# Second selective scan of a two-layer kernel: the sum over states by accumulating DMAs instead of GpSimd additions

## The chip, the cores and the metric

The kernel runs on one core of a Trainium2 chip. The metric is device time in microseconds (us) of one launch; every time below is one core's. The engines are named as in the profile: PE (TensorE matmul), PEld (its weight loads), DVE (VectorE), ACT (ScalarE), POOL (GpSimd), SP (SyncE, which here only issues DMAs); a name with a q (SPq, ACTq, POOLq) is an engine's issuing side.

## What is computed

Two layers run on x (4 sequences of 512 tokens, width 512) and on a context of width 256. Each layer has a selective scan on the context, whose result is gated with x and added to it, and a feed-forward part: in the first layer a mixture of 16 experts (4 chosen for each token) with a shared expert, in the second a ternary-weight block. The part that the change touches is the sum over the 16 states in the second layer's scan:

```python
def step(state, xs):
    d_t, B_t, C_t, u_t = xs
    dA = jnp.exp(d_t[..., None] * A)
    state = state * dA + (d_t * u_t)[..., None] * B_t[:, None, :]
    y_t = jnp.einsum('ben,bn->be', state, C_t)
    return (state, y_t)
...
y = y + D[None, :, None] * u
y = y * jax.nn.silu(z)
```

## The kernel before

The stages run one after another: the first scan (tiles named `ssm_`) beside the splitting of the expert weights, gate and routing (`gate_`), the experts together with the second scan (`moe_`), and the last block (`ffn_`). The change is in the third stage alone.

The second scan. For a batch b the 512 inner channels are 4 chunks of 128 partitions, and a half is 2 chunks. A step s is one half and one of the 16 states n; a batch has 32 steps, and the halves alternate (even steps half 0, odd steps half 1). In a step ACT writes the decay `dA` (two `act_exp` activations, L372), DVE the input `bu` (L449) and then the scan into `hs[:, j]` with j = s % 4 (`dve_scan`, L458; 128 partitions x 1024 f32, 512 KB), and POOL multiplies `hs[:, j]` in place by C (`pool_step`, L491). `pool_add` (L481) then adds `hs[:, j]` to its half of `U`, which held the scan's input u times D (`pool_y_init`, L473) and becomes y. There is one `U` (`dbl` is 1) and there are four `hs` buffers (`R` is 4). Semaphores: `prod_done` counts products, `acc_done` counts additions and starts at 4, and a scan of step s waits for `acc_done` at s + 1, which is the addition of step s - 4.

The slots. The stage is a loop of 168 slots, written out in the same order for every engine, and each slot has work of the experts and one entry of the scan: of a batch's 42 entries the first 10 (`PRO`) prepare the batch (projection, convolution, delta), and the other 32 are its steps. Slots 0 to 87 belong to the shared expert, and 88 to 167 to the 80 tiles of the chosen experts; so the steps of batches 0 and 1 lie beside the shared expert, and those of batches 2 and 3 beside the chosen ones. POOL's queue in a slot is: in the second kind of slot the gather of expert input for the tile after next (`fetch`, L1346, an indirect DMA that POOL issues, 256 KB), then `pool_add` of the step before, then `pool_step` of this one. In a batch's last slot a second `pool_add` follows for step 31.

Around it, `fetch(g + 2)` reads into `xg[:, g % 2]`, which PE transposes (`x_transpose`, L1418) in the next slot. ACT's convolution of the next batch (`act_conv`) writes into `hs` buffers 0 and 1 and waits for additions; ACT issues the store of y (`store_y`, L232) in the third preparing slot of the next batch, for the last batch after its last instruction of the stage. SP loads the weights of an expert as two DMAs of 1088 KB (L1324) and, beside the shared expert, the last block's weights in pieces of 512 KB (L1152).

Of the kernel before, what the change touches and what calls it, by code (L numbers as in the profile page):

```python
# [9 lines left out]
ALU = mybir.AluOpType  # L10
# [9 lines left out]
DI, NS, DC, DR = 512, 16, 4, 16  # L20
# [20 lines left out]
R = 4  # L41
# [4 lines left out]
STEPS = 2 * NS  # L46
# [34 lines left out]
class Mem:  # L81


    def __init__(self, nc, ctx, tag):
        self.nc, self.ctx, self.tag, self.sems = nc, ctx, tag, []
# [20 lines left out]
class Ssm:  # L106
# [10 lines left out]
    def __init__(self, nc, m, l, d, dbl, ring, alone):  # L117
        self.alone = alone
        self.nc, self.l, self.d, self.dbl, self.ring = nc, l, d, dbl, ring
        nsel = NS if alone else 2 * NS  # L120
        self.sel = m.sb("sel", [96, nsel, P], BF16)
        self.cx = m.sb("cx", [P, 2, L])
        self.w_in = m.sb("w_in", [P, 2, DI])
        self.w_x = m.sb("w_x", [P, KC, 96 + DR])
        self.w_up = m.sb("w_up", [P, DI])
        self.cw = m.sb("cw", [P, KC, DC])
        self.cb = m.sb("cb", [P, KC])
        self.db = m.sb("db", [P, KC])
        self.alog = m.sb("alog", [P, KC, NS])
        self.A = m.sb("A", [P, KC, NS])  # L130
        self.Dv = m.sb("Dv", [P, KC])
        self.ident = m.sb("ident", [P, P])
        self.U = m.sb("U", [P, dbl, KC, L])
        self.dlt = m.sb("dlt", [P, dbl, KC, L])
        self.du = m.sb("du", [P, dbl, KC, L])
        self.bc3 = m.sb("bc3", [96, dbl, L], BF16)
        self.low = m.sb("low", [P, L])

        self.Cs = m.sb("Cs", [P, NS if alone else 2, L])
        self.dA = m.sb("dA", [P, ring, HC, L])  # L140
        self.hs = m.sb("hs", [P, R, HC, L])
        if alone:
            self.diagD = m.sb("diagD", [P, KC, P])
        if not alone:
            self.acc = self.hs[:, 0:2, :, :].rearrange("p a b t -> p (a b) t")
            self.tmp = self.hs[:, 2:4, :, :].rearrange("p a b t -> p (a b) t")
        else:
            self.acc = m.sb("acc", [P, KC, L])[:]
            self.tmp = m.sb("tmp", [P, KC, L])[:]


        self.nbu = 2 if alone else 1
        self.bu = m.ps("bu", [P, self.nbu, HC, L])
        self.pB = m.ps("pB", [P, L])
        self.pC = None if alone else self.pB
        self.pY = [m.ps(f"pY{k}", [P, L]) for k in range(HC)] if alone else None
        self.pw = [m.ps("pw", [P, L])[:], self.bu[:, 1, 1, :]] if alone else [self.bu[:, 0, k, :] for k in range(2)]

        self.loaded = m.sem("loaded")
        self.cx_in = m.sem("cx_in")  # L160
        self.a_exp = m.sem("a_exp")
        self.a_neg = m.sem("a_neg")
        self.diag_rdy = m.sem("diag_rdy")
        self.in_rdy = m.sem("in_rdy")
        self.conv_a = m.sem("conv_a")
        self.conv_v = m.sem("conv_v")
        self.u_rdy = m.sem("u_rdy")
        self.xp_rdy = m.sem("xp_rdy")
        self.dts_rdy = m.sem("dts_rdy")
        self.bc_split = m.sem("bc_split")  # L170
        self.dtz_rdy = m.sem("dtz_rdy")
        self.ar_rdy = m.sem("ar_rdy")
        self.e_rdy = m.sem("e_rdy")
        self.t_rdy = m.sem("t_rdy")
        self.q_rdy = m.sem("q_rdy")
        self.ln_rdy = m.sem("ln_rdy")
        self.d_step = m.sem("d_step")
        self.b_rdy = m.sem("b_rdy")
        self.c_rdy = m.sem("c_rdy")
        self.c_evac = m.sem("c_evac")  # L180
        self.cf_rdy = m.sem("cf_rdy")
        self.cd_in = m.sem("cd_in")
        self.cs_in = [m.sem(f"cs_in{n}") for n in range(NS if alone else 0)]
        self.exp_rdy = m.sem("exp_rdy")
        self.bu_done = m.sem("bu_done")
        self.scan_done = m.sem("scan_done")
        self.prod_done = m.sem("prod_done")
        self.acc_done = m.sem("acc_done")
        self.sum_done = m.sem("sum_done")
        self.y_init = m.sem("y_init")  # L190
        self.y_out = m.sem("y_out")
        self.y_dram = m.sem("y_dram")
# [33 lines left out]
    def store_y(self, sp, y_ssm, b):  # L226

        if self.alone:
            sp.wait_ge(self.y_out, 2 * b + 2)
        else:  # L230
            sp.wait_ge(self.acc_done, (b + 1) * STEPS + R)
        sp.dma_start(y_ssm[b * L:(b + 1) * L, :].rearrange("(k p) n -> p k n", p=P),  # L232
                     self.U[:, b % self.dbl, :, :]).then_inc(self.y_dram, 16)

# [83 lines left out]
    def act_conv(self, act, b, c):  # L318
        act.wait_ge(self.in_rdy, b * KC + c + 1)
        if b:  # L320
            act.wait_ge(self.d_step, self.d_count(b, 0))
            if not self.alone:

                act.wait_ge(self.acc_done, b * STEPS + R - 3 + c // 2)
        self.nc.scalar.activation(self.acc[:, c, :], self.bank(b, c), ACT.Identity,
                                  bias=self.cb[:, c:c + 1], scale=self.cw[:, c, DC - 1:DC]).then_inc(self.conv_a, 1)

# [124 lines left out]
    def dve_scan(self, dve, s, j):  # L452

        q = j % self.ring
        dve.wait_ge(self.sum_done if self.alone else self.acc_done, s + 1)
        dve.wait_ge(self.exp_rdy, s + 1)
        dve.wait_ge(self.bu_done, s + 2)
        self.nc.vector.tensor_tensor_scan(self.hs[:, j, :, :].rearrange("p k t -> p (k t)"),  # L458
                                          self.dA[:, q, :, :].rearrange("p k t -> p (k t)"),
                                          self.bu[:, s % self.nbu, :, :].rearrange("p k t -> p (k t)"),  # L460
                                          0.0, ALU.mult, ALU.add).then_inc(self.scan_done, 1)


    def pool_start(self, pool):
        pool.sem_inc(self.prod_done, R)
        if not self.alone:
            pool.sem_inc(self.acc_done, R)

    def pool_y_init(self, pool, b):

# [6 lines left out]
    def pool_add(self, pool, b, half, s, j):  # L477
        Y = self.U[:, b % self.dbl, half * HC:(half + 1) * HC, :]
        pool.wait_ge(self.prod_done, s + 1 + R)
        pool.wait_ge(self.acc_done, s + R)  # L480
        self.nc.gpsimd.tensor_tensor(Y, Y, self.hs[:, j, :, :], ALU.add).then_inc(self.acc_done, 1)  # L481

    def pool_step(self, pool, s, j):
        pool.wait_ge(self.scan_done, s + 1 + self.ring)
# [1801 lines left out]
```

## Time and profile before

| | us |
|---|---|
| median of 3 runs | 2147.91 (2143.99 to 2150.92) |
| the profiled execution, its own time | 2147.24 |
| its span in the trace | 2145.4 |
| PE busy | 1639.1 (76%) |
| DVE busy | 1722.0 (80%) |
| ACT busy | 1205.2 (56%) |
| POOL busy | 1332.6 (62%) |
| the additions, L481, 128 of them | 302.0 (2.36 each) |
| the products of the same scan, L491, 128 of them | 301.6 (2.36 each) |

A busy time counts an instruction's own duration and no waits. Shares over the whole span mix stages with different limits: the steps of the second scan lie at 853 to 1013, about 1070 to 1240, 1320 to about 1525 and 1614 to 1823 us from the start of the span, and only what bounds those stretches matters here. DMAs of every engine's queue run on the same 16 DMA engines in this profile, and a share of DMA is the mean busy share of these 16.

### The profile page before, as it was taken

How to read it: one execution, taken by the hardware profiler on the slowest of the kernel's cores; microseconds unless marked ns; L12 is line 12 of the kernel's file. 1: busy time of each engine (PE TensorE's matmuls, PEld its weight loads, DVE VectorE, ACT ScalarE, POOL GpSimd, SP SyncE). 2: the span in 40 equal slices, each digit the busy share in tenths (PEclk: the TensorE clock that was granted, in tenths of full speed). 3: DMA queues.
4: the chain of work that ended last, by engine and by line, in shares of the span. 5: the costliest groups of instructions: out<-in, count | busy, mean ns of one | idle time of the engine just before them, and what ended most of it. 6: DMA issues, size and time to landing. Idle time of an engine off the chain costs nothing. (4 is left out here: it accounts for less than half of the span.)

```text
span 2145.4 us, 27108 instructions
## 1 busy us (share of the span) xinstructions
PE 1639.1 (76%) x8419; PEld 929.2 (43%) x8442; DVE 1722.0 (80%) x2275; ACT 1205.2 (56%) x1863; POOL 1332.6 (62%) x646
## 2 busy tenths in 40 slices
PE   4465765766664568888888889999999999157788
PEld 1121322222224435666556655666555666023344
DVE  2999999999977645998599947888658888578876
ACT  5776766675643116666666626555465555146576
POOL 2578888788983001998089924888518888663221
PEclk7787988889995569999999999999999999579999
DMA  7537546446546122332322242434444632542200
GB/s 260 196 129 232 178 145 220 165 150 202 177 137 256 69 81 69 110 97 71 106 79 84 72 168 100 167 128 177 152 162 154 213 109 70 178 138 63 74 21 30
DMA packets 121399, 289.21 MB, mean 135 GB/s; under 512 B 22801, under 2 KB 32273, under 8 KB 117073
## 3 DMA queue, kind: packets, MB, share of 16 engines
q1 hardware_dynamic: 86800, 206.73, 28.2%
q0 software_dynamic: 11520, 37.76, 6.0%
q10 hardware_dynamic: 22944, 43.00, 5.4%
q8 instruction: 77, 1.26, 0.2%
q14 instruction: 58, 0.47, 0.1%
HBM read 198.97 MB, written 88.47 MB: 134 GB/s over the span
## 5 line engine op out<-in xcount | busy, mean ns | idle before, releaser
L491 POOL TENSOR_TENSOR ssm_hs<-ssm_hs,ssm_Cs 128x1024 f32<-128x1024 f32 x128 | 313.8, 2461 | 89.3 <-DVE ssm_hs L458 89.3
L491 POOL TENSOR_TENSOR moe_hs<-moe_hs,moe_Cs 128x1024 f32<-128x1024 f32 x128 | 301.6, 2356 | 56.5 <-DVE moe_hs L458 55.6
L458 DVE TENSOR_TENSOR_SCAN moe_hs<-moe_dA,moe_bu 128x1024 f32<-128x1024 f32 x128 | 292.6, 2286 | 22.7 <-ACT moe_dA L372 14.6
L481 POOL TENSOR_TENSOR moe_U<-moe_U,moe_hs 128x1024 f32<-128x1024 f32 x128 | 302.0, 2360 | 6.3
L1445 PE MATMUL moe_pgu<-all_Wreg,moe_xt 128*128 x1920 | 305.1, 313 | 0.0
L458 DVE TENSOR_TENSOR_SCAN ssm_hs<-ssm_dA,ssm_bu 128x1024 f32<-128x1024 f32 x128 | 291.7, 2279 | 0.1
L304 PE MATMUL ssm_pY<-ssm_hs,ssm_ident 128*128 128x512 f32 x512 | 273.0, 661 | 8.6 <-POOL ssm_hs L491 8.5
L1395 PE MATMUL moe_pgu<-all_Wreg 128*128 128x256 f16 x2112 | 252.4, 277 | 3.1 <-DVE moe_hsl L1647 2.8
L1395 PEld LDWEIGHTS moe_pgu<-all_Wreg 128*128 128x128 f16 x2112 | 209.9, 100 | 54.6 <-issue 11.6
L1445 PEld LDWEIGHTS moe_pgu<-all_Wreg,moe_xt 128*128 128x128 f16 x1920 | 188.0, 98 | 96.2 <-issue 2.3
L743 POOL TENSOR_TENSOR ssm_wlo<-ssm_wst,ssm_whi 128x1360 f16<-128x1360 f32 (+2 forms) x63 | 189.2, 3003 | 44.8 <-ACT ssm_wst L678 44.8
L372 ACT ACTIVATE ssm_dA<-ssm_dlt,ssm_A 128x511 f32<-128x511 f32 x256 | 167.9, 709 | 62.0 <-DVE ssm_hs L458 58.9
L282 PE MATMUL ssm_pB<-ssm_bc,ssm_sel 96*128 96x512 bf16 x128 | 55.0, 430 | 170.4 <-DVE ssm_bu L449 170.3
L372 ACT ACTIVATE moe_dA<-moe_dlt,moe_A 128x511 f32<-128x511 f32 x256 | 169.9, 714 | 16.7 <-DVE moe_du L437 16.7
L473 POOL TENSOR_TENSOR moe_U<-moe_U,moe_Dv 128x2048 f32<-128x2048 f32 x4 | 14.4, 3598 | 252.7 <-DVE moe_du L437 252.7
L449 DVE TENSOR_TENSOR ssm_bu<-ssm_du,ssm_pB 128x1024 f32<-128x1024 f32 x128 | 157.0, 1227 | 13.6 <-PE ssm_pB L282 4.2
L1346 POOL DMA_INDIRECT moe_xg<-xn_d,all_idx x80 | 79.3, 991 | 132.5 <-PE moe_px L1418 122.7
L449 DVE TENSOR_TENSOR moe_bu<-moe_du,moe_pB 128x1024 f32<-128x1024 f32 x128 | 156.1, 1220 | 1.3 <-PE moe_pB L282 1.1
L304 PEld LDWEIGHTS ssm_pY<-ssm_hs,ssm_ident 128*128 128x128 f32 x512 | 108.3, 213 | 103.5 <-issue 84.5
L1426 PE MATMUL moe_pys<-all_Wreg,moe_hth 128*128 (+1 forms) x480 | 144.3, 382 | 10.1 <-DVE moe_htl L1665 10.1
L282 PEld LDWEIGHTS ssm_pB<-ssm_bc,ssm_sel 96*128 96x128 bf16 x128 | 12.9, 100 | 269.6 <-DVE ssm_bu L449 254.5
L1546 ACT ACTIVATE moe_sgs<-moe_pgu 128x352 f32<-128x352 f32 x80 | 37.1, 463 | 161.9 <-PE moe_pgu L1445 161.9
(274 smaller groups left out, 3298.8 us busy)
## 6 DMA issues: line engine op xcount, KB each, us to landing
ssm_wst<-in_w_all SPq DMA_DIRECT2D x51, 680.0 KB, 4.9
y_d<-moe_yo ACTq DMA_DIRECT2D x80, 256.0 KB
all_Wreg<-w_hi SPq DMA_DIRECT2D x16, 1088.0 KB
all_Wreg<-w_lo SPq DMA_DIRECT2D x16, 1088.0 KB
w_hi<-ssm_whi SPq DMA_DIRECT2D x51, 340.0 KB, 2.3
w_lo<-ssm_wlo SPq DMA_DIRECT2D x51, 340.0 KB, 3.1
ssm_Cs<-c_d SPq DMA_DIRECT2D x64, 256.0 KB, 5.3
all_Wreg<-w_sh SPq DMA_DIRECT2D x11, 768.0 KB, 9.0
```

The source lines that it names most:

```text
L282: self.nc.tensor.matmul(self.pB[:], self.sel[:, ds(n, 1), :], self.bc3[:, b % self.dbl, :], start=True, stop=True).then_inc(self.b_rdy, 1)
L304: mm = self.nc.tensor.matmul(self.pY[k][:], self.ident[:], self.hs[:, j, k, :], start=False, stop=last, skip_group_check=True)
L372: ex = nc.scalar.activation(self.dA[:, q, k, 1:L], self.dlt[:, b % self.dbl, c, 1:L], ACT.Exp, scale=self.A[:, c, ds(n, 1)])
L449: self.nc.vector.tensor_tensor(self.bu[:, s % self.nbu, :, :], self.du[:, b % self.dbl, half * HC:(half + 1) * HC, :], self.pB[:].unsqueez ...
L458: self.nc.vector.tensor_tensor_scan(self.hs[:, j, :, :].rearrange("p k t -> p (k t)"), self.dA[:, q, :, :].rearrange("p k t -> p (k t)"), ...
L481: self.nc.gpsimd.tensor_tensor(Y, Y, self.hs[:, j, :, :], ALU.add).then_inc(self.acc_done, 1)
L491: self.nc.gpsimd.tensor_tensor(self.hs[:, j, :, :], self.hs[:, j, :, :], self.Cs[:, i:i + 1, :].to_broadcast([P, HC, L]), ALU.mult)\
L743: nc.gpsimd.tensor_tensor(wlo[:, k, 0:n], wst[:, k, 0:n], whi[:, k, 0:n], ALU.subtract).then_inc(lo_rdy, 1)
L1346: nc.gpsimd.indirect_dma_start(out=xg[:, g % 2, :], out_offset=None, in_=r["xn_d"], in_offset=bass.IndirectOffsetOnAxis(ap=r["idx"][:, g:g ...
L1395: mm = nc.tensor.matmul(pgu[u % 2][:, q * TS:(q + 1) * TS], Ws[:, shared_place(c), z, o:o + P], xs[:, t % 2, k, :], start=(k == 0 and z == ...
L1426: mm = nc.tensor.matmul(py[:], ht[0:n, q, :], w_of(w, z, n, HK * 2 * IE + q * H, H), start=(q == 0 and z == 0 and ht is hth), stop=(q == 2 ...
L1445: mm = nc.tensor.matmul(ps, xt[:, g % 2, k, :], w_of(w, z, P, k * 2 * IE + o, IE), start=(k == 0 and z == 0 and xt is xth), stop=(k == HK ...
```

## The change

`pool_add` becomes a DMA from `hs[:, j]` to its half of `U`, both in SBUF, with an addition at the destination, issued by POOL. In place of `acc_done` there is a semaphore for each half, `acc_in[half]`, which every such DMA raises by 16 when it has landed. A DMA waits for the one before it of its own half, that is of step s - 2; a scan waits for the DMA of step s - 4; the store of y and the convolution of the next batch wait for both semaphores.

```diff
-        self.acc_done = m.sem("acc_done")
+        self.acc_in = [m.sem(f"acc_in{h}") for h in range(2)]
...
         else:
-            sp.wait_ge(self.acc_done, (b + 1) * STEPS + R)
+            for h in range(2):
+                sp.wait_ge(self.acc_in[h], 16 * (b + 1) * NS)
...
-                act.wait_ge(self.acc_done, b * STEPS + R - 3 + c // 2)
+                act.wait_ge(self.acc_in[0], 16 * (b * NS - 1))
+                act.wait_ge(self.acc_in[1], 16 * (b * NS - 2 + c // 2))
...
-        dve.wait_ge(self.sum_done if self.alone else self.acc_done, s + 1)
+        if self.alone:
+            dve.wait_ge(self.sum_done, s + 1)
+        elif s >= R:
+            dve.wait_ge(self.acc_in[s % 2], 16 * ((s - R) // 2 + 1))
...
         pool.sem_inc(self.prod_done, R)
-        if not self.alone:
-            pool.sem_inc(self.acc_done, R)
...
         pool.wait_ge(self.prod_done, s + 1 + R)
-        pool.wait_ge(self.acc_done, s + R)
-        self.nc.gpsimd.tensor_tensor(Y, Y, self.hs[:, j, :, :], ALU.add).then_inc(self.acc_done, 1)
+        if s >= 2:
+            pool.wait_ge(self.acc_in[half], 16 * (s // 2))
+
+        pool.dma_start(Y, self.hs[:, j, :, :], accum_op=ALU.add).then_inc(self.acc_in[half], 16)
```

POOL's queue beside the chosen experts, before: a gather, an addition that waits for the addition before it, a product that waits for its scan, and again (the gather's semaphore has the name that its number had in the first stage).

```order
L1346 DMA moe_xg<-xn_d,all_idx 128x512 [waits ssm0_y_out]
L481 TENSOR_TENSOR moe_U<-moe_U,moe_hs 128x1024 [waits moe_acc_done,moe_prod_done]
L491 TENSOR_TENSOR moe_hs<-moe_hs,moe_Cs 128x1024 [waits moe_c_evac,moe_scan_done]
L1346 DMA moe_xg<-xn_d,all_idx 128x512 [waits ssm0_y_out]
L481 TENSOR_TENSOR moe_U<-moe_U,moe_hs 128x1024 [waits moe_acc_done,moe_prod_done]
L491 TENSOR_TENSOR moe_hs<-moe_hs,moe_Cs 128x1024 [waits moe_c_evac,moe_scan_done]
```

The same place of POOL's queue in the changed kernel.

```order
L1351 DMA moe_xg<-xn_d,all_idx 128x512 [waits ssm0_sum_done]
L486 DMA moe_U<-moe_hs 128x1024 [waits moe_acc_in1,moe_prod_done]
L496 TENSOR_TENSOR moe_hs<-moe_hs,moe_Cs 128x1024 [waits moe_c_evac,moe_scan_done]
L1351 DMA moe_xg<-xn_d,all_idx 128x512 [waits ssm0_sum_done]
L486 DMA moe_U<-moe_hs 128x1024 [waits moe_acc_in0,moe_prod_done]
L496 TENSOR_TENSOR moe_hs<-moe_hs,moe_Cs 128x1024 [waits moe_c_evac,moe_scan_done]
```

No instruction has changed its place. The addition is now a DMA on the same queue as the gathers, with the gather of each slot ahead of it, and its wait is for a DMA of two steps before (`acc_in0` and `acc_in1` in turn), ahead of the product.

## Rows read from the trace of the kernel before

**Rows 1.** Busy time by engine in three stretches of steps (columns in the first line).

```profile
core 0: us, PE busy (x) PEld busy (x) DVE busy (x) ACT busy (x) POOL busy (x), PEclk, DMA share, GB/s
900.00:1000.00 100.00, 88.29 (x638) 62.33 (x637) 94.50 (x111) 63.15 (x122) 94.11 (x41) 0.98 0.29 90
1350.00:1500.00 150.00, 150.00 (x947) 94.63 (x945) 128.50 (x163) 80.51 (x173) 131.28 (x70) 1.00 0.44 156
1640.00:1800.00 160.00, 159.15 (x1005) 100.48 (x1004) 136.37 (x170) 85.47 (x185) 139.68 (x74) 1.00 0.44 149
```

**Rows 2.** The additions: durations, and the lists of waits before and behind them.

```profile
L481 POOL TENSOR_TENSOR moe_U<-moe_U,moe_hs x128: 2339/2359/2377, 858.2 to 1822.9; 128x1024 f32<-128x1024 f32 x128
its engine sat idle before it (us, times) until:
who waited for it (us, times):
busy tenths in 40 slices 0000000000000000444034400333203333000000
```

**Rows 3.** Timeline of one slot beside the shared expert.

```profile
908.49 2.29 DVE L458 TENSOR_TENSOR_SCAN moe_hs<-moe_dA,moe_bu 128x1024 f32<-128x1024 f32 x1 [0.27 <-ACT moe_dA L372]
908.50 2.35 POOL L481 TENSOR_TENSOR moe_U<-moe_U,moe_hs 128x1024 f32<-128x1024 f32 x1
...
910.69 0.40 DVE L1639 SCALAR_TENSOR_TENSOR moe_sgs<-moe_sgs,moe_pgu 128x256 f32<-128x256 f32 x1
910.85 2.35 POOL L491 TENSOR_TENSOR moe_hs<-moe_hs,moe_Cs 128x1024 f32<-128x1024 f32 x1
911.12 0.43 DVE L1642 SCALAR_TENSOR_TENSOR moe_pgu<-moe_pgu,moe_sgs 128x256 f32<-128x256 f32 x1
...
911.59 0.37 ACT L1532 CAST moe_hsh<-moe_pgu 128x256 f16<-128x256 f32 x1 [1.40 <-DVE moe_pgu L1642]
911.86 1.33 ACT L372 ACTIVATE moe_dA<-moe_dlt,moe_A 128x511 f32<-128x511 f32 x2
...
913.28 2.29 DVE L458 TENSOR_TENSOR_SCAN moe_hs<-moe_dA,moe_bu 128x1024 f32<-128x1024 f32 x1 [0.27 <-ACT moe_dA L372]
```

**Rows 4.** Timeline of one slot beside the chosen experts.

```profile
1646.12 0.99 POOL L1346 DMA_INDIRECT moe_xg<-xn_d,all_idx  x1
...
1647.00 0.60 PE L1418 MATMUL moe_px<-moe_ident,moe_xg 128*128 128x128 f32 x4
1647.12 2.37 POOL L481 TENSOR_TENSOR moe_U<-moe_U,moe_hs 128x1024 f32<-128x1024 f32 x1
...
1650.13 2.35 POOL L491 TENSOR_TENSOR moe_hs<-moe_hs,moe_Cs 128x1024 f32<-128x1024 f32 x1 [0.64 <-DVE moe_hs L458]
...
1652.64 0.98 POOL L1346 DMA_INDIRECT moe_xg<-xn_d,all_idx  x1 [0.15 <-issue]
...
1653.73 0.60 PE L1418 MATMUL moe_px<-moe_ident,moe_xg 128*128 128x128 f32 x4
```

**Rows 5.** What PE waited for beside batches 2 and 3 (us, times, longest).

```profile
PE moe_px L1418 <- DMA moe_xg<-xn_d,all_idx: 2.5, 2, 1.6
```

**Rows 6.** DMA from 1646 to 1652 us in 40 slices: a gather and a store.

```profile
DMA  0000000000007972799899961000000000000000
...
q0 software_dynamic: 80, 0.26, 14.5%
q10 hardware_dynamic: 144, 0.26, 11.7%
```

**Rows 7.** DMA issues beside the shared expert (last column: issue to landing).

```profile
wq_d<-moe_tq ACTq DMA_DIRECT2D x24, 256.0 KB, 2.0
...
moe_yo<-in_w_gate SPq DMA_DIRECT2D x5, 512.0 KB, 3.7
```

**Rows 8.** SP's waits for an expert's weights to land.

```profile
SPq L1326 <- DMA all_Wreg<-w_lo: 129.9, 15, 10.4
```

**Rows 9.** Timeline at the end of the stage.

```profile
1822.91 2.34 POOL L481 TENSOR_TENSOR moe_U<-moe_U,moe_hs 128x1024 f32<-128x1024 f32 x1
...
1828.00 0.45 ACTq L232 DMA_DIRECT2D y_ssm<-moe_U  x1
1837.41 0.34 SPq L1838 DMA_DIRECT2D ffn_ident<-in_ident_bf  x1
```

## The prediction, made before the changed kernel ran

> **What bounds the kernel now.** I read the busy time by stretch first, then the list of who waits for the additions, then the timeline of one slot of each kind.
>
> Beside the chosen experts (batches 2 and 3) PE is busy 150.00 of 150 us and 159.15 of 160 [rows 1]: it sets the pace, one slot in 1652.64 - 1646.12 = 6.52 us [rows 4], and POOL has slack: its product idles 0.64 us until the scan ends [rows 4]. Beside the shared expert (batches 0 and 1) no engine is full: DVE is busy 94.50, POOL 94.11 and PE 88.29 of 100 us [rows 1]. There the slot is a loop of DVE and ACT. From one scan's start to the next: 2.20 us to L1639, 0.43 to L1642, 0.47 to ACT's cast, 0.27 to the decays and 1.42 until these are done and the next scan starts, together 4.79 [rows 3]. The scan's last wait is for ACT, 0.27 us. POOL's addition and product take 2.35 each and, with 0.08 us between product and addition, also fill 4.79 [rows 3], but POOL follows the scan and no engine holds for it: under "who waited for it" of the additions stands nothing [rows 2]. So 302 us of POOL's time go away where they cost nothing.
>
> **The change part by part.**
>
> *Removed:* 128 additions of 2.36 us [rows 2]. Nobody waited for them, so 0. Lower bound of the effect: if POOL does hold the loop after all, see the third rival.
>
> *Added on POOL:* 128 issues. The trace has no such issue; the nearest row is the gather's, 0.99 us [rows 4]. Beside the shared expert POOL then has 1.0 + 2.35 = 3.4 us in a slot of 4.79, beside the chosen experts one gather more, 4.3 of 6.52. Even twice that issue time fits (4.4 and 5.3). The cover is POOL's slack behind the scan; without it each further us would go to every step. 0 us.
>
> *Added on the DMA engines:* per step 512 KB that is read, added and written from SBUF to SBUF. The trace shows neither an accumulating nor an SBUF-to-SBUF transfer. In the window of a slot the store of 256 KB from SBUF takes 11.7% of 6 us, 0.70 us of all 16 engines, the gather 14.5%, 0.87 us [rows 6]; so one pass of 512 KB is 1.4 us by the store and 1.7 by the gather. An addition must read source and destination: two passes, 2.8 us, if the write overlaps the reads as it does in a store. Lower bound, one pass: 1.4. Upper bound, three passes one after another: 4.2. I take 2.8, because reads and writes overlap in every transfer shown. The engines are otherwise busy 0.29 x 4.79 = 1.4 us of a slot beside the shared expert and 0.44 x 6.52 = 2.9 beside the chosen ones [rows 1], so they get to 4.2 of 4.79 and to 5.7 of 6.52. They hold, with little to spare.
>
> The Trainium skill ("Collectives: The Full Stack", the part on the bandwidth ceiling) says that an addition inside a DMA engine costs nothing by itself, but needs a second source read on the same ring, so that it goes at half the rate of a copy. No row here shows it; by it the transfer would be the same 2.8 us, and the three passes of the upper bound would be out.
>
> *From issue to landing.* The gather issued at 1646.12 has its first bytes moving in the 13th of 40 slices of 0.15 us, at 1647.8, 1.7 us after the start of its issue [rows 4, 6]. A store of 256 KB lands 2.0 us after its issue [rows 7], 1.3 more than its 0.70 on the engines; a load of 512 KB from HBM lands after 3.7, 2.3 more than its pass of 1.4. The new transfer ends in SBUF but comes from SBUF too, so I take the store's 1.3; with the load's 2.3 the landing is at 6.8. So an accumulating DMA lands 1.7 + 2.8 + 1.3 = 5.8 us after its issue starts; bounds 4.4 and 7.2. If a load of equal weight runs beside it, its 2.8 double: 8.6.
>
> *The new waits.* DMA s waits for DMA s - 2 of its half, two slots before: 9.58 us beside the shared expert, 13.0 beside the chosen ones, against 5.8 to 8.6. Behind the waiting DMA on POOL stand the product of the next step and the next gather; for the product wait the DMA after it, the copies of C and four steps later the scan, for the gather waits PE. Nothing of it moves while the landing stays under 9.58. A scan waits for the DMA of s - 4, issued some 14 us before: 0. The convolution of the next batch and the stores of batches 0 to 2 come three slots or more after the DMAs that they wait for: 0. With them the extra cost of the steps is 0.
>
> *The gathers* go ahead of the DMA of their slot and behind that of the slot before, 5.5 us older. From a gather's issue to its transposes are 1653.73 - 1646.12 = 7.6 us [rows 4], and it needs 1.7 + 0.87 + 1.3 = 3.9; PE waited for one only twice, 2.5 us in all [rows 5]. 0 us; the third of the mechanisms that make it slower is here.
>
> *The end.* The one place with no slot after it: the last addition ran from 1822.91 to 1825.25, ACT issued the store of y at 1828.00, and the next stage opened at 1837.41, after that store [rows 9]. The last DMA is issued at 1822.9 and lands at 1822.9 + 5.8 = 1828.7: the store goes 0.7 us later (bounds 0 and, with 7.2, 2.1), and the stage with it.
>
> **Sum.** 0 for the steps + 0.7 for the end. Against the profiled execution's own 2147.24 us that is 2147.9; its own time is 0.67 below the median of the runs, 2147.91, so I predict 2148.6.
>
> The Trainium skill ("DMA: Bandwidth & Descriptors", Anatomy of one DMA) gives 2.0 us plus the bytes at 436 GB/s, which makes an estimate of 4.4 us for two passes of 512 KB and, with 1.0 for the issue, 5.4; by it the end term would be 0.3 instead of 0.7. No row here shows the constant.
>
> **The rivals.**
>
> 1. *The DMA engines run full.* For it: 0.29 and 0.44 of them are already in use [rows 1], and beside an expert's two weight loads they have no room. It decides from 3.4 us of engine time per addition beside the shared expert (4.79 - 1.4) and 3.6 beside the chosen ones. At the upper bound of 4.2 the slots become 5.6 and 7.1 us: 64 x 0.8 + 64 x 0.6 = about 88 us, 2236. Against: it needs reads and writes that don't overlap. Chance 0.22.
>
> 2. *The chain of a half.* Engine time is there, but a DMA takes over 9.58 us to land, and POOL stands in its wait with the product behind it. With doubled transfers of the upper bound, 1.7 + 8.4 + 1.3 = 11.4, a step takes 5.7 instead of 4.79: 64 x 0.9 = 58 us, 2206. For it: latency per DMA is the least known term. Against: 7.2 alone, even at the bound. Chance 0.10.
>
> 3. *Late gathers.* While an expert's weights load (15 waits, 129.9 us, 8.7 each, the longest 10.4 [rows 8]) the DMA before a gather needs 8.6 us instead of 5.8, is still 3 us from done when the gather is queued behind it, and the gather shares too: 3.9 + 0.9 + 3 = 7.8 against 7.6. PE, the bound there, would wait perhaps 1 us per gather in the load, and each load covers one or two: some 16 us, 2164. Against: it is at the edge, and loads cover only part of the slots. Chance 0.12.
>
> 4. *Faster: POOL holds the loop beside the shared expert.* For it: its 2.35 + 2.35 + 0.08 are the very 4.79 of the slot, and scan and addition start within 0.01 us of each other [rows 3]. Freed, the slot would fall to DVE's busy share, 0.945 x 4.79 = 4.53: 64 x 0.26 = 17 us, 2131. It decides if the scans start on an addition; against it stands that the list of its waiters is empty [rows 2] and that the DVE and ACT loop closes by itself. Chance 0.08.
>
> **How the numbers follow.** The forecast, no change beyond the end term, has 0.48, with a range of its own of 2144 to 2153. Differences up to 0.3% (6.4 us) a measurement of this kernel can't tell from none. Faster is rival 4, 0.08. Slower are rivals 1 and 2 and most of rival 3, 0.42. The rest, 0.50, is the same. The range reaches down to 2141 and up to the bound of the first rival, 2236; outside lie rival 4 and what is worse than my bounds, together under 0.2.
>
> **What would show it.** POOL's busy time falls by about 302 us less the issues, 1 us each (or by all, if these aren't counted); the share of its queue q0 rises by 128 x 2.8 us; the slot in a timeline stays 4.79 and 6.5; the scans still wait last for ACT; no wait of POOL for a DMA; the store at 1828.7 on this clock. Wrong is it if POOL waits for the accumulating DMA, if the DMA share in the steps is near 1, or if the products start at once and the slot is under 4.79.

## The result, and the profile after

The changed kernel takes 2165.2 us (median of 5 runs, 2163.0 to 2168.1) against 2150.9 for the kernel before on the same chip: a ratio of 1.0076, 95% interval 1.0057 to 1.0094. It is slower by 0.76%, some 16 us (the two medians are 14.3 us apart). The forecast was no change (2148.6). The time lies within the stated range, outside of the likeliest case's own, 2144 to 2153, and at the size of the third rival, late gathers (2164).

The changed kernel in the three stretches of [rows 1], busy time by engine:

```profile
core 0: us, PE busy (x) PEld busy (x) DVE busy (x) ACT busy (x) POOL busy (x), PEclk, DMA share, GB/s
900.00:1000.00 100.00, 88.33 (x639) 62.38 (x638) 94.50 (x111) 63.29 (x122) 64.55 (x40) 0.98 0.87 197
1350.00:1500.00 150.00, 144.81 (x897) 89.52 (x895) 122.05 (x155) 77.30 (x165) 96.11 (x66) 1.00 0.84 228
1640.00:1800.00 160.00, 157.00 (x978) 97.65 (x975) 132.46 (x166) 82.60 (x178) 102.41 (x70) 1.00 0.86 236
```

POOL lost 30 of 100 us, as it should. Beside the shared expert nothing else moved: DVE has its 94.50 again. Beside the chosen experts PE, which sets the pace there, is no longer full: 144.81 of 150 where it had 150.00. The DMA share went from 0.29 beside the shared expert and 0.44 beside the chosen ones to 0.87 and to 0.84 and 0.86; the prediction's sums were 4.2 of 4.79 and 5.7 of 6.52, 0.88 and 0.87.

The new transfers, those that waited for one, and the queue of POOL in the page:

```profile
L486 POOL DMA_DIRECT2D moe_U<-moe_hs x128: 870/890/1108, 858.6 to 1841.2; - x128
...
  DVE moe_hs L463: 5.7, 22
  POOL moe_hs L496: 2.3, 1
  POOL moe_xg L1351: 0.3, 2
...
q0 software_dynamic: 29952, 104.88, 22.6%
```

An issue takes 0.89 us. The queue's share was 6.0% of 2145.4 us before, so one accumulating DMA of 512 KB takes (0.226 x 2163.1 - 0.060 x 2145.4) / 128 = 2.8 us of all 16 engines, the term that was assumed. The 22 waits of scans are in the place where they waited for ACT before, 0.27 us each, and cost nothing: the 64 scans beside the shared expert start within 0.1 us of those of before. Of POOL's one wait for an add, 2.3 us at 1718.45, the product's own scan explains all but 0.03 us.

**Where the time went.** I laid the starts of TensorE's `down` (L1431, the experts' second product, early in each slot) of both timelines side by side. By the clock of the kernel before, the changed kernel is 0.04 us behind at 1332 us, 10.0 behind at 1535 (end of batch 2), 9.9 at 1609, 12.7 at 1638 and 18.1 at 1821. What PE waited for in that part, after:

```profile
PE moe_px L1423 <- DMA moe_xg<-xn_d,all_idx: 5.4, 7, 1.6
PE moe_pys L1431 <- issue: 3.7, 8, 1.3
PE moe_pB L283 <- issue: 1.3, 5, 0.4
```

The first line is [rows 5] with seven waits in place of two. The other two have no counterpart before. One late gather in the timeline:

```profile
1352.80 1.06 POOL L1351 DMA_INDIRECT moe_xg<-xn_d,all_idx  x1 [0.16 <-issue]
...
1353.66 0.60 PE L1423 MATMUL moe_px<-moe_ident,moe_xg 128*128 128x128 f32 x4
1353.82 1.01 POOL L486 DMA_DIRECT2D moe_U<-moe_hs  x1
...
1361.60 0.66 PE L1423 MATMUL moe_px<-moe_ident,moe_xg 128*128 128x128 f32 x4 [1.04 <-DMA moe_xg<-xn_d,all_idx]
```

The gather issued at 1352.80 feeds the transposes of the next slot, 8.8 us later where 7.6 was the slack, and the weights of an expert load in these same microseconds. Ahead of it in POOL's queue stood an add that was issued together with these loads:

```profile
1347.23 0.32 SPq L1329 DMA_DIRECT2D all_Wreg<-w_hi  x1
...
1347.32 1.02 POOL L486 DMA_DIRECT2D moe_U<-moe_hs  x1
```

The trace's semaphore events tell when it landed: 12.7 us after its issue, where an add beside the shared expert took 5.4 (median). Each of the six gathers that made PE wait in batch 2 stood behind such an add. These six adds took 12.0 to 13.2 us, had 6.4 to 7.7 us to go when the gather was issued, and the gather landed 1.2 to 1.8 us after them, 8.0 to 9.0 us after its own issue. (The seventh wait is at 1545 us, between the batches, where the kernel before has one too.) In the window from 1353 to 1362 us the DMA engines are 90% busy or nearly so in most slices:

```profile
DMA  9899899697998989989949999699899896998999
...
q0 software_dynamic: 314, 1.16, 56.8%
q1 hardware_dynamic: 162, 1.14, 31.7%
q10 hardware_dynamic: 281, 0.51, 15.6%
```

q0 carries POOL's transfers, q1 the weights, q10 the stores of `y_d`. Six slots of batch 2 with such a wait each came out 0.9 to 1.6 us longer, 7.8 together; 4.8 of this lie ahead of the transposes, and 2.9 behind them, where the second kind of loss sits. This second kind has no releaser:

```profile
1696.80 1.50 PE L1450 MATMUL moe_pgu<-all_Wreg,moe_xt 128*128 x9
...
1699.62 0.23 PEld L1431 LDWEIGHTS moe_pys<-all_Wreg,moe_hth 128*128 128x128 f16 x2 [1.68 <-issue]
1699.63 0.60 PE L1431 MATMUL moe_pys<-all_Wreg,moe_hth 128*128 x2 [1.32 <-issue]
```

TensorE has ended one slot and begins the next 1.3 us late, though nobody it waits for is late. Between L1450 and L1431 (or L283) stand in its program the two reads of the routing table `tab` from SBUF into registers (`value_load`, which weights and which place). Most of these gaps are 0.2 to 0.4 us. The trace has the reads themselves, with their duration in ns (min/median/max), before and then after:

```profile
L1473 PEldq TENSOR_LOAD <-all_tab x80: 296/316/1004, 1259.2 to 1812.9; - x80
L1474 PEldq TENSOR_LOAD <-all_tab x80: 294/302/566, 1260.0 to 1813.6; - x80
```

```profile
L1478 PEldq TENSOR_LOAD <-all_tab x80: 296/608/1675, 1259.2 to 1830.8; - x80
L1479 PEldq TENSOR_LOAD <-all_tab x80: 295/666/1237, 1260.0 to 1832.1; - x80
```

A read takes twice as long beside the adds. Ahead of the gap above, the second read alone took 1.24 us. And there is a third piece, the clock at the start of batch 3, after and then before:

```profile
1628.00:1638.00 10.00, 9.44 (x42) 5.57 (x43) 6.70 (x10) 2.80 (x6) 8.55 (x6) 0.68 0.45 109
```

```profile
1628.00:1638.00 10.00, 10.00 (x67) 6.44 (x66) 8.93 (x12) 4.86 (x12) 8.43 (x5) 1.00 0.87 328
```

TensorE was granted 0.68 of its 2.4 GHz there, so it spent part of the stretch at 1.2; the slot took 2.8 us more. It had waited 3.1 us for DVE just before, in both kernels. Three runs below without a DMA add in this place fell too: 0.75 over 10 us with the adds beside the shared expert alone, 0.93 over 10 with no add, 0.89 over 30 in the kernel before with the table as constants. So I count these 2.8 us of the profile's 17.7 as no part of the change.

The last DMA add was issued at 1841.25 and the store of y at 1846.17, 4.9 us later; in [rows 9] it was 5.1 after the addition's start. The last add had landed at 1845.8, before the store. The end costs nothing.

### The profile page after: what moved, and what is told of

The parts are those of the page before. It is cut to its first block and busy times, and to the rows that moved or that the text cites. A ratio compares the mean times of both kernels' runs of the same rounds, so it can differ in the third digit from the quotient of the medians.

```text
span 2163.1 us, 27146 instructions
## 1 busy us (share of the span) xinstructions
PE 1652.8 (76%) x8442; PEld 929.6 (43%) x8442; DVE 1722.2 (80%) x2275; ACT 1206.6 (56%) x1863; POOL 1152.2 (53%) x646
## 5 line engine op out<-in xcount | busy, mean ns | idle before, releaser
L1450 PE MATMUL moe_pgu<-all_Wreg,moe_xt 128*128 x1920 | 305.5, 313 | 0.0
L305 PE MATMUL ssm_pY<-ssm_hs,ssm_ident 128*128 128x512 f32 x512 | 277.5, 669 | 8.0 <-POOL ssm_hs L496 7.9
L1450 PEld LDWEIGHTS moe_pgu<-all_Wreg,moe_xt 128*128 128x128 f16 x1920 | 188.2, 98 | 96.4 <-issue 2.3
L283 PE MATMUL ssm_pB<-ssm_bc,ssm_sel 96*128 96x512 bf16 x128 | 56.3, 439 | 165.0 <-DVE ssm_bu L451 165.0
L1431 PE MATMUL moe_pys<-all_Wreg,moe_hth 128*128 (+1 forms) x480 | 146.0, 386 | 13.9 <-DVE moe_htl L1670 10.1
L486 POOL DMA_DIRECT2D moe_U<-moe_hs x128 | 120.3, 940 | 21.6 <-POOL moe_hs L496 20.1
L283 PEld LDWEIGHTS ssm_pB<-ssm_bc,ssm_sel 96*128 96x128 bf16 x128 | 12.9, 101 | 265.0 <-DVE ssm_bu L451 248.8
```

Of the source, the lines that this page charges most:

```text
L283: self.nc.tensor.matmul(self.pB[:], self.sel[:, ds(n, 1), :], self.bc3[:, b % self.dbl, :], start=True, stop=True).then_inc(self.b_rdy, 1)
L305: mm = self.nc.tensor.matmul(self.pY[k][:], self.ident[:], self.hs[:, j, k, :], start=False, stop=last, skip_group_check=True)
L486: pool.dma_start(Y, self.hs[:, j, :, :], accum_op=ALU.add).then_inc(self.acc_in[half], 16)
L1431: mm = nc.tensor.matmul(py[:], ht[0:n, q, :], w_of(w, z, n, HK * 2 * IE + q * H, H), start=(q == 0 and z == 0 and ht is hth), stop=(q == 2 ...
L1450: mm = nc.tensor.matmul(ps, xt[:, g % 2, k, :], w_of(w, z, P, k * 2 * IE + o, IE), start=(k == 0 and z == 0 and xt is xth), stop=(k == HK ...
```

## Experiments

Three theories stood against each other. T1: late gathers are the loss. T2: the load on the DMA engines delays other things too; of these T2a, the register reads, and T2b, TensorE's instructions. T3: POOL's issue and its waits. Ratios are to the kernel before, run beside each group of experiments on the same chip: its median was 2145.9 us for the first four, 2149.3 for the next four (constants, both together, the decays first on the kernel before), 2147.2 for the three after them and 2146.9 for the last. The groups ran on different chips, so ratios are compared and not times. A ratio is good to some 0.15 points, and a difference of two to 0.2 or 0.25, some 5 us; the single microseconds below have to be read so.

### Adds by DMA beside the shared expert alone

```diff
-        pool.dma_start(Y, self.hs[:, j, :, :], accum_op=ALU.add).then_inc(self.acc_in[half], 16)
+        if b < 2:
+            pool.dma_start(Y, self.hs[:, j, :, :], accum_op=ALU.add).then_inc(self.acc_in[half], 16)
+        else:
+            ...
+            self.nc.gpsimd.tensor_tensor(Y, Y, self.hs[:, j, :, :], ALU.add).then_inc(self.acc_pool, 1)
```

> The adds go by DMA only in batches 0 and 1 (beside the shared expert); in batches 2 and 3 (beside the chosen experts) GpSimd adds again, in one chain. All theories that read the loss from the traces (the starts of the scan part only after 1360 us) expect the time of the kernel before: 2151 within 3 us. If the DMAs also cost something that the profiled execution of one chip hid, or if freeing GpSimd beside the shared expert had a worth, it would be outside of that: 2158 if half of the 14 us is lost there.

2146.1 us, ratio 1.0002 (0.9990 to 1.0014). The whole loss is beside the chosen experts, though the DMA share beside the shared expert is as high. The two reads of the table are fast again as well, 320 and 302 ns in the median. One stretch of each kind:

```profile
900.00:1000.00 100.00, 87.55 (x642) 61.88 (x641) 94.94 (x111) 63.38 (x123) 65.26 (x41) 1.00 0.87 197
1640.00:1800.00 160.00, 158.84 (x1000) 100.07 (x999) 136.02 (x171) 85.77 (x185) 138.97 (x75) 1.00 0.44 147
```

### Gathers one slot earlier

```diff
+        xgb = [xg[:, 0, :], xg[:, 1, :], hshl[:].rearrange("p a b -> p (a b)")[:, 0:2 * H].bitcast(F32)]
...
-                    if 0 <= g < NSTEP - 2:
+                    if g == 0:
+                        pool.wait_ge(s_dn, NU)
+                        fetch(2)
+                    if 0 <= g < NSTEP - 3:
                         pool.wait_ge(tx_rdy, g + 1)
-                        fetch(g + 2)
+                        fetch(g + 3)
```

> The changed kernel with a third buffer for the gathered tokens (it takes the place of the shared expert's hidden tiles, which are done by then), so each gather is issued one slot, 6.5 us, earlier before its transposes. Theory 1, late gathers are the loss: the six jumps at late gathers add up to 7.8 us in the profile, so 2157 (all 14 us back, 2151, if they are the whole loss). Theory 2, the DMA engines' load delays other things too (TensorE's starts with no releaser shown, stores of y_d): only 4 us back, the waits seen for the gathers themselves, 2161. Theory 3, GpSimd's own issue and waits: nothing back, 2165.

2152.7, ratio 1.0031 (1.0017 to 1.0046). 0.45% of the 0.76% came back, 9.7 us, near T1's 8 and less than all. No wait for a gather is left; the starts without a releaser are:

```profile
PE moe_pys L1435 <- issue: 1.6, 3, 0.9
...
PE moe_pB L283 <- issue: 1.2, 2, 1.0
```

T1 is the larger part of the loss and not all of it; T3, which expected nothing back, is out.

### A plain copy in place of the add

```diff
-        pool.dma_start(Y, self.hs[:, j, :, :], accum_op=ALU.add).then_inc(self.acc_in[half], 16)
+        pool.dma_start(Y, self.hs[:, j, :, :]).then_inc(self.acc_in[half], 16)
```

> The accumulating DMA becomes a plain copy from SBUF to SBUF of the same 512 KB with the same waits and queue (y is then the last product of each half and no sum). Traffic of the read for the add gone, latency and issue kept. If the load on the 16 DMA engines is what costs (theories 1 and 2), engine time per add falls from 2.8 us towards 1.4 and the loss of 14 us falls by more than half: 2151 to 2157. If it is GpSimd's issue or the wait on landings (theory 3): 2163 to 2165.

2149.5, ratio 1.0021 (1.0006 to 1.0035). The queue and the waits are the same, and 0.55% is gone: it is the load. Issued together with an expert's weights, a copy landed after 10.0 to 11.7 us in batch 2, and the gather behind it after 6.7 to 7.7, about when PE wants it. The second read of the table took 340 ns in the median, in place of 666. The page gives this kernel's q0 and the landing:

```profile
q0 software_dynamic: 29952, 104.88, 14.1%
...
moe_U<-moe_hs POOLq DMA_DIRECT2D x128, 512.0 KB, 3.8
```

The 3.8 is the median over the whole kernel; beside the shared expert alone it is 3.2, against 5.4 for the add.

(0.141 x 2147.3 - 0.060 x 2145.4) / 128 = 1.36 us of all engines for the copy, against 2.8 for the add, although both move the same bytes by the page. The copy is the one pass of 1.4 that stood as lower bound, and an add costs two. The rule of the Trainium skill that the prediction weighed ("Collectives: The Full Stack", the bandwidth ceiling: an addition goes at half the rate of a copy) is what these two runs show.

### No add at all

```diff
-        pool.dma_start(Y, self.hs[:, j, :, :], accum_op=ALU.add).then_inc(self.acc_in[half], 16)
+        pool.sem_inc(self.acc_in[half], 16)
```

> The adds are left out altogether: neither GpSimd nor a DMA adds, y is only u times D. GpSimd has only the products and the gathers. My account (GpSimd is not waited for) expects the time of the kernel before, 2151 within 3 us, or 2 us less where two late gathers of before vanish. If GpSimd's freed time were worth something and the DMA hid it: under 2145.

2144.2, ratio 1.0000 (0.9988 to 1.0011). Without any addition on POOL the kernel takes the same time, within some 2.5 us: the 302 us that the change frees could not have made this kernel faster, whatever the DMA cost.

### The routing table as constants, after and before

```diff
-                    return Wx[0:k, ds(w, 1), z, o:o + n].rearrange("p o n -> p (o n)")
+                    return Wx[0:k, w, z, o:o + n]
...
-                        ws[g] = pe.value_load(r["tab"][0:1, 1, g:g + 1], min_val=0, max_val=WR - 1)
-                        need = pe.value_load(r["tab"][0:1, 0, g:g + 1], min_val=1, max_val=E)
+                        need = NEED[g]
+                        ws[g] = need % WR
```

> The changed kernel, but TensorE no longer reads the two entries of the routing table (which expert's weights, which of three places) from SBUF into registers at each slot's start; they stand in the program as constants of this input. Beside late gathers the profile of after has starts of down or of the B spread that come 0.2 to 1.3 us late with no releaser (issue), all just behind those two reads. Theory 2a, the reads take longer beside the DMA load: those starts are on time again, about 5 to 7 of the 16 us come back, ratio to before 1.004 to 1.005. Theory 2b, TensorE's instructions themselves arrive late: nothing changes, 1.0076.

> The same constants in the kernel before, as the control. Under theory 2a the reads are hidden there but for a few starts: 0 to 2 us less, ratio 0.999 to 1.000. If the constants save time by themselves (fewer instructions, static addresses), it shows here: under 0.998, and the previous run has to be read against this one.

After with constants: 2160.1, ratio 1.0047 (1.0031 to 1.0062); 0.29% came back, 6.2 us, little more than the uncertainty of such a difference. Before with constants: 1.0005 (0.9991 to 1.0019), nothing. So T2a holds: the reads cost nothing in the kernel before and some 6 us beside the adds, where the trace shows them at twice their length. Among PE's waits of the changed kernel with constants no start of `down` or of the spread without releaser is left, and the late gathers stay:

```profile
PE moe_px L1424 <- DMA moe_xg<-xn_d,all_idx: 9.1, 7, 4.8
PE moe_px L1424 <- issue: 0.2, 1, 0.2
```

The edit also makes the addresses of the weights static. But the spread of B over the partitions (L283), whose address never hung on the table, started late as well, and it stands right behind the reads; so I put it down to the reads. Fewer instructions and static addresses by themselves gain nothing in the kernel before, which has the same edit; that they gain only beside the load isn't excluded.

### Both together

The constants and the third buffer.

> Constants and the third buffer for the gathers together, in the changed kernel. If late gathers and late register reads are the whole loss: the time of the kernel before with constants, ratio 0.999 to 1.001. If a third thing is left (stores of y_d, weights, instructions), it keeps 2 us or more: 1.002 or higher; with theory 2b 1.003, as with the third buffer alone.

2151.0, ratio 1.0006 (0.9993 to 1.0020). The loss is gone, with every DMA add still made:

```profile
1350.00:1500.00 150.00, 150.00 (x946) 94.62 (x945) 128.47 (x162) 80.26 (x173) 100.85 (x70) 1.00 0.87 236
1640.00:1800.00 160.00, 160.00 (x1008) 100.89 (x1007) 136.61 (x173) 86.32 (x186) 108.60 (x75) 1.00 0.86 235
...
ACT moe_yo L1562 <- DMA y_d<-moe_yo: 4.9, 5, 1.5
```

PE is full in both stretches at a DMA share of 0.87 and 0.86. The stores of `y_d` land late here too (ACT waits 4.9 us for them), and that costs nothing. 9.7 and 6.2 us one by one, 15 together: two causes that add up. The step from the third buffer alone to both, 1.0031 to 1.0006, measures the reads a second time: 0.25%.

### The decays first

The loop beside the shared expert invited another edit, on the kernel before:

```diff
-                    if g <= 0 and slot:
-                        sh_high(slot - 1)
                     if s is not None:
                         ...
                         S.act_exp(act, b, half, s, n, s % R)
+                    if g <= 0 and slot:
+                        sh_high(slot - 1)
```

> A try at a better version, on the kernel before: ScalarE computes a step's dA ahead of the high half of the shared expert's hidden tile, and not behind it. Beside the shared expert the scan waited 0.27 us for ScalarE in each slot of 4.79, and ScalarE itself waited 1.2 us for VectorE before that high half. If the scan then waits for VectorE's own work alone, a slot shrinks to about 4.5: 0.27 x 64 = 17 us less, 2129, ratio 0.992. If the high half, now later, holds VectorE or TensorE back instead: no gain, 1.000 or above.

2139.5, ratio 0.9947 (0.9930 to 0.9964). DVE hardly waits for ACT any more (0.4 us in two waits of its scans, 14.6 in 51 before), and scans follow each other at 4.42 us in a plain slot (915.65 to 920.07). From the first to the last scan of a batch, with the slots that carry more of DVE's work, the mean fell from 5.01 to 4.80 and from 4.97 to 4.72 us, 14 us in two batches. POOL (below) was now as full as DVE, so I asked whether DMA adds would be worth something on this base.

> ScalarE's dA first, and the adds by DMA beside the shared expert alone (batches 0 and 1). In the run with dA first on the kernel before, VectorE no longer waited for ScalarE, but GpSimd's two passes of 2.36 us now stood end to end, 4.74 us per slot, so the slot fell from 4.79 only that far. With the add by DMA GpSimd needs 2.35 + 0.9 = 3.25 us per slot and VectorE's own 4.5 bounds it. If that is the account: another 0.2 us x 64 = 13 us, ratio to before 0.989 to 0.990, 2126. If GpSimd was not the bound there: 0.9947 as without the DMAs, 2138.

2131.9, ratio 0.9938 (0.9915 to 0.9962), not told apart from the run without the DMA adds, and far from 0.989. From 900 to 1000 us, first without and then with them:

```profile
900.00:1000.00 100.00, 89.88 (x660) 63.52 (x658) 97.37 (x115) 67.84 (x130) 97.69 (x43) 1.00 0.32 98
```

```profile
900.00:1000.00 100.00, 90.47 (x669) 64.56 (x667) 97.38 (x115) 65.66 (x125) 67.69 (x42) 1.00 0.88 200
```

POOL fell from 97.69 to 67.69 and DVE stayed at 97.37 and 97.38. Mean scan distances were 4.80 and 4.72 again. My expectation took an engine that is full for the bound; DVE was equally full, and without the DMA adds no scan waited for an addition. That the ring of four tiles let POOL catch up in the slots in which DVE has more to do is my reading and not shown.

> The change as it is, with dA first: the 13 us that DMA adds give beside the shared expert, and the 16 us that they cost beside the chosen experts. Ratio 0.989 + 0.0076 = 0.997; if GpSimd was not the bound beside the shared expert: 0.9947 + 0.0076 = 1.002.

2150.9, ratio 1.0025 (1.0012 to 1.0038): against 0.9947 without the change, it costs 0.78% on this base as well.

> dA first, adds by DMA beside the shared expert alone, and the third buffer for the gathers. In the kernel before two gathers are late beside the chosen experts, 1.6 and 0.8 us of wait. If an early gather takes these away: 2 to 4 us less than without it, ratio 0.988; if other things take their place, the same as without it, 0.989 to 0.990.

2135.8, ratio 0.9950 (0.9932 to 0.9968): no gain from early gathers where no adds go by DMA beside the chosen experts. The simplest of the faster versions is the kernel before with the decays first.

### The landing of an add

```diff
         pool.dma_start(Y, self.hs[:, j, :, :], accum_op=ALU.add).then_inc(self.acc_in[half], 16)
+        pool.wait_ge(self.acc_in[half], 16 * (s // 2 + 1))
```

> The changed kernel, but GpSimd waits right behind each accumulating DMA until it has landed, before it starts the next product, so that the time from issue to landing can be read (in the kernel as changed no one waits for a landing last). My prediction took 5.8 us (4.4 to 7.2), and 8.6 beside a load of an expert's weights. By 5.8 GpSimd needs 2.35 + 1.0 + 5.8 = 9.1 us per slot beside the shared expert against 4.8, and 9.1 against 6.5 beside the chosen experts, 64 slots each: 275 + 165 = 440 us more, 2605. By 4.4: 2430; by 7.2: 2785.

2549.6 us, ratio 1.187, between the figures for 4.4 and 5.8. POOL's waits also thin out the load: the DMA share is 0.53 and 0.55 beside the two kinds of experts, in place of 0.87. Where POOL waits, the trace shows the landing (min, median, max); over all adds:

```profile
DMA to landing us min/median/max: 4.5/5.3/12.7
```

Beside the shared expert the median is 5.3, beside the chosen ones 5.6. The gathers landed in 3.7 us there, with no add in flight ahead of them. The estimate from the Trainium skill in the prediction ("DMA: Bandwidth & Descriptors", Anatomy of one DMA), 5.4 with the issue, agrees with the 5.3, and with the 5.4 beside the shared expert in the changed kernel. It does not hold beside an expert's load: there the changed kernel's adds took 12.0 to 13.2.

## Why the prediction was right in its range and wrong in its account

The time fell inside the stated range, but the likeliest case, no change, did not come true, and what it rests on failed in one step, the gathers.

**The additions were not waited for, 0 us:** right. Without any add the kernel takes the same time (1.0000), and the scans beside the shared expert start where they did. Rival 4, POOL holding that loop, is refuted by the same run, and once more by the run in which POOL stood at 97.69 of 100 and still did not bind.

**The issue, 1.0 us:** 0.88 beside the shared expert, 1.01 beside the chosen ones. Right.

**The engine time, 2.8 us:** 2.8, and the shares 0.88 and 0.87 came out as 0.87 and 0.86. Right; the copy's 1.36 confirms that an add is two passes. Rival 1 needed 3.4.

**The landing, 5.8 us (8.6 beside a load):** the 5.8 is good, the 8.6 is not. The medians are 5.4 beside the shared expert and 7.2 in batch 2 of the changed kernel, and the adds issued with an expert's weights took 12.0 to 13.2. (The 5.8 counts a part twice: the 1.3 that a store takes beyond its bytes already holds its start, and the 1.7 of the gather's start is added to it.) The chain of a half (rival 2) did not bind even so, because beside the chosen experts it has 13.0 us: POOL waited for an add once in the whole kernel, and by 0.03 us more than for the scan.

**"The gathers ... 0 us":** this is the step that failed. The slack of 7.6 us from issue to transposes was good, and so was the need of 3.9 for a gather that has the queue and the engines to itself: 3.7 measured where no add was in flight. But the same text had put the engines at 0.87, and behind an add that shares them with an expert's weights a gather took 8.0 to 9.0 us. Seven gathers came too late for PE, where two had. Earlier gathers gave 9.7 us back. The rival of late gathers had the mechanism and the place, the load of an expert's weights, and a size of 16 us. It gave the add ahead 8.6 us and 3 to go, where 12.0 to 13.2 and 6.4 to 7.7 were measured; that it stood at 0.12 "at the edge" was the misjudgment, since 7.8 against 7.6 by its own sum says even odds.

**What no step and no rival had:** TensorE's register reads from SBUF, 6.2 us. The prediction looked for transfers that the load could delay and not for other accesses. That the size of rival 3 (2164) was met is partly luck: its gathers alone are worth some 10 us, and the other 6 came from the reads. Shown is that the reads take twice as long beside the adds, and that they cost time only there; what makes them slow, a busy SBUF or its way out, stays open. Nor was it tried what delays a gather more, the add ahead of it in its queue or the share of the engines. The copy, with the same queue and half the engine time, still shows two waits for a gather, no more than before, so a place in the queue alone is not enough.

**The end, 0.7 us:** 0. The last add landed 4.5 us after its issue, within the 4.9 in which the last tile's store was prepared anyway.

The forecast's "third rival" for POOL holding the loop is the fourth of its list.

## What to carry to other kernels

A resource at 0.87 is not "holding": add up the mean load, and then ask for each transfer with a deadline what is left of its slack when every engine is busy, because the transfers with short slack fail first, here at a mean of 0.87. Look for the moment at which several transfers are issued together: the mean hides it, and all six late gathers of batch 2 stood behind one. Look beyond the transfers, too: whoever reads SBUF with nothing queued to hide it (here two register reads at the head of each slot) can be late when the DMA load rises. And free an engine only if somebody waits for it: leaving the work out altogether is a cheap run that says what the best possible offload is worth, here nothing.

## What the runs showed of the hardware

- An accumulating DMA of 512 KB from SBUF to SBUF takes 2.8 us of all 16 engines and landed 5.4 us after its issue beside the shared expert; the plain copy of the same bytes takes 1.36 and landed there after 3.2. Issued together with two loads of 1088 KB (six times in batch 2), the add took 12.0 to 13.2 us and the copy 10.0 to 11.7. The page counts the same bytes and packets for both, so its GB/s shows half of the add's load and its busy share all of it.
- TensorE's reads of two registers from SBUF take 0.32 and 0.30 us (medians) and are hidden in the kernel before, at a DMA share of 0.44 (constants gain nothing, 1.0005). With the adds, at 0.84 to 0.86, they take 0.61 and 0.67 us, up to 1.7, and cost some 6 us over 80 slots.
- At the same point of the program, behind the same wait, TensorE's granted clock over some 10 us was between 0.68 and 1.00 in different runs, with and without the change: a difference of nearly 3 us between two profiles that belongs to neither kernel.
